# A recommender kernel on one core: each copied 256-byte row is landed as four 64-byte runs

## The chip, the cores and the metric

The kernel runs on one core of a Trainium2 chip. The metric is the device time of one execution in microseconds (us), the median of several runs. A core has five engines with a queue each: TensorE (PE), VectorE (DVE), ScalarE (ACT), GpSimd (POOL) and SyncE (SP). DMAs are issued from the queues of SP, ACT and POOL and are carried out by 16 DMA engines that all of them share.

## What is computed

```python
x = relu(dense @ Wb0 + bb0)            # dense: 2048 x 13, Wb0: 13 x 512
x = relu(x @ Wb1 + bb1)                # 512 x 256
d = relu(x @ Wb2 + bb2)                # 256 x 64
sp = emb[arange(26)[None, :], sparse_idx]      # 26 tables of 12500 rows of 64 floats
T = concatenate([sp, d[:, None, :]], axis=1)   # 27 vectors of 64 for each sample
Z = einsum('bnd,bmd->bnm', T, T)
h = concatenate([d, Z[:, li, lj]], axis=1)     # the 351 pairs below the diagonal
h = relu(h @ Wt0 + bt0)                # 415 x 512
h = relu(h @ Wt1 + bt1)                # 512 x 256
p = sigmoid(h @ Wt2 + bt2)             # 2048 outputs
```

All of it is in float32. Each sample reads 26 rows of 256 bytes from places in device memory that its indices name: 2048 x 26 = 53,248 rows.

## The kernel before

**Steps.** The batch is worked off in eight steps of 256 samples. The tile `rows` has 128 partitions; a partition holds two samples of the step (halves h = 0 and 1, 64 floats each) for each of 26 tables.

**Gathers.** Tables 0 to 24 are fetched by POOL with indirect DMAs. One takes a table and a half, 128 rows (`gather`, L376 to L380), so a step has 50 and the kernel 398 in all, issued one behind the other. `begin` holds a run of gathers until TensorE has read what it overwrites.

**Copied rows.** Table 25 (`FETCHED`) is fetched row by row with plain DMAs whose source address is read from the tile `fetch_at`: the SP queue copies the 128 rows of half 0 of a step (L335 to L341), the ACT queue those of half 1 (L758 to L764). Each copy is 256 bytes into one partition of `fetched`. A step's 128 rows on a queue are issued as four parts of 32; ahead of a part stands `keep_pace`, a wait that holds the part of number n until the gathers have come to about column 11 n (50 columns to a step), and `load_places`, a load of 32 addresses into registers (L288). `fetched` has a place of its own for each of the eight steps. DVE moves a step's 128 x 128 block into `rows` (`move_fetched`, L833 to L838) once all 256 rows have landed.

**The last step** is cut finer, so that little is left to do once the last gather lands. Half 0 of all tables comes first, with table 24 of half 1, then half 1 of tables 0 to 15 (`LAST_RUNS`). Of half 1 of tables 16 to 23 there are eight "late" tiles of 128 rows, numbered l = 0 to 7 = 2q + k, q being a quarter of the samples. Six of them are gathered by POOL (L402 to L406). The two with q = 2, `COPIED_Q`, that is l = 4 and l = 5, are copied row by row instead: l = 4 by the SP queue (L343 to L348), l = 5 by the ACT queue (L766 to L771), in four parts of 32 each and without `keep_pace`, from the time that step 6 has been transposed. They land straight in `rows`.

**TensorE** transposes what has landed (`turn` L444, `turn_last` L467, `turn_late` L479), DVE (in the last step ACT too) spreads the transposed vectors into `vecs_st` and `vecs_mv` (`spread` L844, `spread_last` L849, `spread_late` L853 and L718), TensorE forms the 27 x 27 products (L494, L510, `gram_quarter` L529), DVE transposes and packs the pairs (L871 to L886), and TensorE carries them through the top layers (L561 to L609). The PE order at the end of the last step is written out by hand: `turn_late(0)`, `turn_late(1)`, `gram_quarter(0)`, `turn_late(2)`, `turn_late(3)`, `gram_quarter(1)`, `turn_late(4)`, `turn_late(5)`, `turn_late(6)`, and so on, with filler matmuls (`stay_busy`, L539) between. `turn_late(l)` also waits for the spread of the tile two before it. DVE's order there is `spread_last(11)`, then `spread_late(1)`, (3), (5), (7); ACT has the even ones.

Of the kernel before, what the change touches and what calls it, by code (L numbers as in the profile page):

```python
# [34 lines left out]
U8 = mybir.dt.uint8  # L35

P = 128
# [3 lines left out]
DIM = 64  # L41
# [4 lines left out]
STEPS = BATCH // STEP  # L46
# [22 lines left out]
FETCHED = TABLES - 1  # L69
# [5 lines left out]


ROW_BYTES = 4 * DIM
PARTS = 4
PART = P // PARTS

# [14 lines left out]
COPIED_Q = 2  # L95
# [22 lines left out]
def build(nc, x, idx, fetch_idx, emb, wb0, bb0, wb1, bb1, wb2, bb2, wt0, wt1, bt1, wt2, bt2, out):  # L118
# [3 lines left out]
    with ExitStack() as ctx:  # L122
        def sb(name, shape, dt=F32):
            return ctx.enter_context(nc.sbuf_tensor(name, shape, dt))
# [4 lines left out]
        def sem(name):  # L129
            return ctx.enter_context(nc.semaphore(name))  # L130
# [23 lines left out]
        fetch_neg = sb("fetch_neg", [2 * PARTS, (STEPS + 1) * PART], I32)  # L154
        fetch_at = sb("fetch_at", [2 * PARTS, (STEPS + 1) * PART], I32)
        late_fetch_base = sb("late_fetch_base", [2 * PARTS, PART], I32)
        fetched = sb("fetched", [P, STEPS, 2 * DIM])

        x_t = sb("x_t", [DENSE, BATCH])
        hb0 = sb("hb0", [P, B0 // P, CHUNK])  # L160
# [37 lines left out]
        fetch_idx_loaded = sem("fetch_idx_loaded")  # L198
        fetch_done = sem("fetch_done")
        fetch_landed = [[sem(f"fetch_landed{h}_{i}") for i in range(STEPS)] for h in range(2)]  # L200
        late_fetch_landed = [sem(f"late_fetch_landed{k}") for k in range(LATE_TILES)]
        late_fetch_base_ready = sem("late_fetch_base_ready")
        fetched_moved = sem("fetched_moved")
# [70 lines left out]
        def late_rows(q, k):  # L274

            return rows[:, LATE + LATE_TILES * q + k, :]
# [16 lines left out]

        def late_landing(k, p):

            return late_rows(COPIED_Q, k)[p:p + 1, DIM:].bitcast(U8)

        def landing(i, h, p):
            return fetched[p:p + 1, i, h * DIM:(h + 1) * DIM].bitcast(U8)

        turned_tiles = [bank[0:PAIR_ROWS, 0, :] for bank in (ps_feat[1], ps_turn[0], ps_turn[1])]

# [20 lines left out]
        @block.sync  # L323
        def _(sp):
            sp.dma_start(idx_raw[:, 0:STEP_COLS], idx[:, 0:STEP_COLS]).then_inc(idx_loaded, 16)
            sp.dma_start(fetch_raw[:, :], fetch_idx).then_inc(fetch_idx_loaded, 16)
            sp.dma_start(idx_raw[:, STEP_COLS:], idx[:, STEP_COLS:]).then_inc(idx_rest_loaded, 16)
            sp.dma_start(wb0_sb[:, :], wb0).then_inc(bottom_loaded, 16)
            sp.dma_start(wb1_sb[:, :, :], wb1.rearrange("(k p) n -> p k n", p=P)).then_inc(bottom_loaded, 16)
            sp.dma_start(wb2_sb[:, :, :], wb2.rearrange("(k p) n -> p k n", p=P)).then_inc(bottom_loaded, 16)  # L330
            sp.dma_start(wt0_sb[:, :, :], wt0.rearrange("k p n -> p k n")).then_inc(top_loaded, 16)
            sp.dma_start(wt1_sb[:, :, :], wt1.rearrange("(k p) n -> p k n", p=P)).then_inc(top_loaded, 16)

            sp.wait_ge(fetch_done, 5)
            for i in range(STEPS):  # L335
                for q in range(PARTS):
                    keep_pace(sp, i * PARTS + q)
                    places = load_places(mybir.EngineType.SP, 0, q, i)
                    for j in range(PART):
                        sp.dma_start(landing(i, 0, q * PART + j), emb_bytes[bass.ds(places[j], ROW_BYTES)])\  # L340
                            .then_inc(fetch_landed[0][i], 16)  # L341

            sp.wait_ge(rows_turned, STEPS * NR)  # L343
            for jj in range(4):
                places = load_places(mybir.EngineType.SP, 0, jj, STEPS)
                for j in range(PART):
                    sp.dma_start(late_landing(0, jj * PART + j), emb_bytes[bass.ds(places[j], ROW_BYTES)])\
                        .then_inc(late_fetch_landed[0], 16)  # L348

            sp.wait_ge(probs_ready, 1)  # L350
            sp.dma_start(out.rearrange("(p n) -> p n", p=P), probs[:, :]).then_inc(out_stored, 16)
            sp.wait_ge(out_stored, 16)
# [56 lines left out]
        def _(pe):  # L409
# [60 lines left out]
            def turn_late(l):  # L470

                q, tile = LATE_RUNS[l]
                k = LAST_NR + l
                if q == COPIED_Q:
                    pe.wait_ge(late_fetch_landed[tile], 16 * P)
                else:
                    pe.wait_ge(late_landed[l], 16)
                wait_spread(k - 2)
                nc.tensor.transpose(ps_turn[k % 2][:, 0, :], late_rows(q, tile), ident[:, :]).then_inc(rows_turned, 1)  # L479
# [235 lines left out]
        def _(act):  # L715
# [42 lines left out]
            for i in range(STEPS):  # L758
                for q in range(PARTS):
                    keep_pace(act, i * PARTS + q)  # L760
                    places = load_places(mybir.EngineType.Activation, 1, q, i)
                    for j in range(PART):
                        act.dma_start(landing(i, 1, q * PART + j), emb_bytes[bass.ds(places[j], ROW_BYTES)])\
                            .then_inc(fetch_landed[1][i], 16)  # L764

            act.wait_ge(rows_turned, STEPS * NR)  # L766
            for jj in range(4):
                places = load_places(mybir.EngineType.Activation, 1, jj, STEPS)
                for j in range(PART):
                    act.dma_start(late_landing(1, jj * PART + j), emb_bytes[bass.ds(places[j], ROW_BYTES)])\  # L770
                        .then_inc(late_fetch_landed[1], 16)  # L771

            last_step()
# [7 lines left out]
        def _(dve):  # L781
# [51 lines left out]
            def move_fetched(i):  # L833

                for h in range(2):
                    dve.wait_ge(fetch_landed[h][i], 16 * P)
                dve.wait_ge(rows_turned, i * NR + NR)
                nc.vector.tensor_copy(rows[:, FETCHED, :], fetched[:, i, :]).then_inc(fetched_moved, 1)  # L838

            def spread(i, r):  # L840

# [108 lines left out]
            def last_step():  # L950
                i = STEPS - 1
                spread_last(0)
                place_d_last()
                relu_low(i - 1, 0)
                relu_high(i - 1, 0)
                spread_last(1)
                spread_last(2)
                logit(i - 1, 0)
                relu_low(i - 1, 1)
                relu_high(i - 1, 1)  # L960
                spread_last(3)
                spread_last(4)
                logit(i - 1, 1)
                copy_d_last()
                move_fetched(i)
                spread_last(5)
                spread_last(6)
                turn_gram(i, 0)
                pack(i, 0)
                spread_last(7)  # L970
                move_feat(i, 0)
                spread_last(8)
                relu_low(i, 0)
                spread_last(9)
                relu_high(i, 0)
                spread_last(10)
                logit(i, 0)
                spread_last(11)
                spread_late(1)
                spread_late(3)  # L980
                spread_late(5)
                spread_late(7)
                turn_gram_last()
                pack_last()
                move_feat_last()
                relu_high(i, 1, top_0_blocks_last(1))
                logit(i, 1)
# [112 lines left out]
```

## Time and profile before

| | us |
|---|---|
| median of 3 runs | 526.32 |
| lowest and highest | 524.11 and 526.5 |
| the profiled execution's own time | 525.22 |
| its span in the trace | 523.5 |

Busy shares of the span: POOL 72%, PE 60%, DVE 49%, ACT 1%. The 16 DMA engines move 32 GB/s in the mean. Shares are means over stages; what an edit is worth is read from the chain that ended last and from who waits for whom in the stage that it touches. The sequencers' own time (issuing DMAs, loading registers) is not counted as busy and is read by line.

### The profile page before, as it was taken

To read this page: it belongs to the slowest core of one execution; us is meant where nothing else is said; L and a number is where in the kernel's file an instruction comes from. 1 tells how busy PE (TensorE), PEld (TensorE's weight loads), DVE (VectorE), ACT (ScalarE), POOL (GpSimd) and SP (SyncE) were. 2 spreads that over 40 slices of the span, in tenths; PEclk is the share of its full clock that TensorE was granted. 3 is DMA by queue.
4 is the path that set the end of the run, shared out by engine and by line. 5 is a ranking of instruction groups with operands and counts; after the bars stand their busy time and mean duration, and the time that the engine had idled before them with its cause. 6 is when DMAs were issued, how large, how long until landed. Compare 5 with 4: busy or idle time off the path is not lost.

```text
span 523.5 us, 12507 instructions
## 1 busy us (share of the span) xinstructions
PE 315.0 (60%) x3386; PEld 230.2 (44%) x3386; DVE 254.3 (49%) x391; ACT 4.7 (1%) x11; POOL 377.6 (72%) x405
## 2 busy tenths in 40 slices
PE   3799983764372655561555834638438445497887
PEld 1233433652271535441354622626237233486765
DVE  5433866782463434822357344543446433543423
ACT  1000000000000000000000000000000000000001
POOL 5777777777777777777777777777777777777730
PEclk9978996695576765866558665676657676779589
DMA  6445324444354432454324443444323443333410
GB/s 210 33 27 30 28 30 28 30 28 28 30 29 29 27 30 28 29 28 28 28 29 28 29 27 29 27 29 29 27 28 29 27 30 29 27 27 30 31 16 3
DMA packets 20412, 16.87 MB, mean 32 GB/s; under 512 B 12163, under 2 KB 13452, under 8 KB 20345
## 3 DMA queue, kind: packets, MB, share of 16 engines
q0 software_dynamic: 12736, 13.07, 31.6%
q1 hardware_dynamic: 4634, 2.72, 4.3%
q10 hardware_dynamic: 2988, 0.54, 3.3%
q14 instruction: 42, 0.34, 0.3%
q8 instruction: 12, 0.20, 0.2%
HBM read 16.28 MB, written 0.01 MB: 31 GB/s over the span
## 4 chain that ended last, share of the span: by engine, by line
POOL 64%; issue 22%; PE 9%; DMA 2%; DVE 2%; POOLq 0%; ACT 0%; DVEq 0%; ACTq 0%
POOL rows L378 64%; PE ps_t L422 3%; DMA rows<-in_emb,idx_row 2%; PE ps_turn L430 1%; PE ps_feat L539 1%; PE ps_feat L413 1%; PE ps_gram L413 1%; DMA idx_raw<-in_idx 1%; PE ps_gram L529 1%; DVE hb L786 1%; PE ps_t L609 0%; PE ps_turn L479 0%; PE ps_t L561 0%; DVE vecs_mv L1030 0%; PE ps_feat L561 0%
## 5 line engine op out<-in xcount | busy, mean ns | idle before, releaser
L378 POOL DMA_INDIRECT rows<-in_emb,idx_row x392 | 370.1, 944 | 122.6 <-issue 119.0
L444 PE MATMUL ps_turn<-ident,rows 128*128 128x128 f32 x182 | 39.9, 358 | 140.0 <-DMA rows<-in_emb,idx_row 131.2
L844 DVE COPY vecs_st<-ps_turn 128x512 f32<-128x512 f32 (+1 forms) x49 | 47.0, 959 | 107.3 <-PE ps_turn L444 106.9
L844 DVE COPY vecs_mv<-ps_turn 64x512 f32<-64x512 f32 (+1 forms) x98 | 96.1, 981 | 0.7
L444 PEld LDWEIGHTS ps_turn<-ident,rows 128*128 128x128 f32 x182 | 25.9, 177 | 153.9 <-issue 145.6
L494 PE MATMUL ps_gram<-vecs_mv,vecs_st 128*32 128x54 f32 x1792 | 42.7, 286 | 29.3 <-DVE vecs_mv L844 15.2
L494 PEld LDWEIGHTS ps_gram<-vecs_mv,vecs_st 128*32 128x32 f32 x1792 | 39.3, 164 | 34.1 <-DVE vecs_mv L844 18.0
L609 PE MATMUL ps_t<-wt_sb,ht_t 128*128 128x256 f32 x128 | 51.3, 570 | 0.0
L609 PEld LDWEIGHTS ps_t<-wt_sb,ht_t 128*128 128x128 f32 x128 | 34.9, 286 | 15.1 <-issue 8.1
L878 DVE STREAM_TRANSPOSE gram_s<-ps_gram 128x864 f32<-128x864 f32 x15 | 16.2, 1083 | 49.5 <-PE ps_gram L494 42.2
L588 PE MATMUL ps_t<-feat_t,wt_sb 117*128 117x128 f32 x180 | 36.7, 362 | 0.2 <-DVE feat_t L890 0.2
L588 PEld LDWEIGHTS ps_t<-feat_t,wt_sb 117*128 117x128 f32 x180 | 34.6, 280 | 0.5 <-DVE feat_t L890 0.5
L422 PE MATMUL ps_t<-hb,wb_sb 128*128 128x512 f32 x64 | 32.1, 659 | 3.1 <-DVE hb L786 3.1
L588 PE MATMUL ps_feat<-feat_t,wt_sb 117*128 117x128 f32 x180 | 25.2, 276 | 0.0
L588 PEld LDWEIGHTS ps_feat<-feat_t,wt_sb 117*128 117x128 f32 x180 | 23.0, 195 | 0.0
L422 PEld LDWEIGHTS ps_t<-hb,wb_sb 128*128 128x128 f32 x64 | 13.3, 214 | 22.0 <-issue 17.3
L570 PE MATMUL ps_feat<-ident,feat 128*117 128x128 f32 x45 | 11.1, 366 | 17.6 <-DVE feat L886 17.6
L905 DVE SCALAR_TENSOR_TENSOR ht_w<-ps_t,wt_sb 128x256 f32<-128x256 f32 x16 | 6.8, 425 | 25.0 <-PE ps_t L609 25.0
L599 PE MATMUL ps_t<-bt_sb,ones 1*128 1x256 f32 x32 | 16.9, 621 | 0.0
L570 PEld LDWEIGHTS ps_feat<-ident,feat 128*117 128x117 f32 x45 | 7.7, 233 | 20.4 <-DVE feat L886 19.5
L582 PE MATMUL ps_t<-d_t,wt_sb 65*128 65x128 f32 x60 | 16.6, 372 | 0.0
L582 PEld LDWEIGHTS ps_t<-d_t,wt_sb 65*128 65x128 f32 x60 | 15.0, 292 | 1.0
(86 smaller groups left out, 238.2 us busy)
## 6 DMA issues: line engine op xcount, KB each, us to landing
fetched<-in_emb SPq DMA_DIRECT2D x1024, 0.2 KB
fetched<-in_emb ACTq DMA_DIRECT2D x1024, 0.2 KB
rows<-in_emb,idx_row POOLq DMA_INDIRECT x398, 3.7
rows<-in_emb SPq DMA_DIRECT2D x128, 0.2 KB
rows<-in_emb ACTq DMA_DIRECT2D x128, 0.2 KB
wt_sb<-in_wt SPq DMA_DIRECT2D x1, 1024.0 KB
wb_sb<-in_wb SPq DMA_DIRECT2D x1, 512.0 KB
wt_sb<-in_wt SPq DMA_DIRECT2D x1, 512.0 KB
```

The source lines that it names most:

```text
L378: nc.gpsimd.indirect_dma_start(rows[:, t, h * DIM:(h + 1) * DIM], None, emb_rows, bass.IndirectOffsetOnAxis(idx_row[:, c:c + 1], 0)).then_ ...
L413: nc.tensor.matmul(ps_b0[m], wb0_sb[:, m * P:(m + 1) * P], x_t[:, bass.ds(c * CHUNK, CHUNK)], start=True, stop=True).then_inc(b0_summed, 1)
L422: summed = nc.tensor.matmul((ps_t0, ps_t1)[m][:, :], wb1_sb[:, k, m * P:(m + 1) * P], hb0[:, k, :], start=(k == 0), stop=(k == B0 // P - 1))
L444: turned = nc.tensor.transpose(ps_turn[r % 2][:, j, :], rows[:, first + j, :], ident[:, :])
L494: summed = nc.tensor.matmul(ps_gram[32 * v:32 * v + 32, b, g * 2 * VECS:(g + 1) * 2 * VECS], vecs_st[:, c, :], vecs_mv[:, c, :, :].rearran ...
L570: turned = nc.tensor.transpose(ps_feat[u][0:PAIR_ROWS, k, :], feat[:, u, k * PAIR_ROWS:(k + 1) * PAIR_ROWS], ident[:, :])
L582: nc.tensor.matmul(top_0_blocks(u, m // 2)[:, m % 2, :], wt0_sb[0:D_ROWS, PAIR_TILES, m * P:(m + 1) * P], d_t[:, u, :], start=True, stop=F ...
L588: summed = nc.tensor.matmul(top_0_blocks(u, m // 2)[:, m % 2, :], wt0_sb[0:PAIR_ROWS, k, m * P:(m + 1) * P], feat_t[:, u, k, :], start=Fal ...
L599: nc.tensor.matmul(ps_t1[:, 0:T1], ones[0:1, :], bt1_sb[:, :], start=True, stop=False)
L609: summed = nc.tensor.matmul(ps_t1[:, 0:T1], ht0_t[:, k, :], wt1_sb[:, k, :], start=False, stop=(k == T0 // P - 1))
L844: moved = nc.vector.tensor_copy(to, source)
L878: nc.vector.transpose(gram_s[u][:, 0:VECS * SLOTS], unit_products(VECS)).then_inc(gram_turned, 1)
```

## The change

A copied row is described to the DMA as four pieces of 16 floats (64 bytes). In `fetched` a sample's row used to be one run of 64 floats; now the tile is laid out piece, half, 16 floats, so that the four pieces of one row stand 32 floats apart. `move_fetched` puts them back into order while it moves them. The late rows used to land in `rows` directly; now they land in a tile of their own, `late_copied`, in which the pieces of the two tiles alternate, and DVE moves each tile into `rows` with a copy of its own (`move_late_copied`), placed between `spread_late(3)` and `spread_late(5)`. `turn_late` of the two tiles waits for that move in place of the landing.

```diff
+PIECES = 4
+PIECE = DIM // PIECES
...
-        fetched = sb("fetched", [P, STEPS, 2 * DIM])
+        fetched = sb("fetched", [P, STEPS, PIECES, 2, PIECE])
+        late_copied = sb("late_copied", [P, PIECES, LATE_TILES, PIECE])
...
-            return late_rows(COPIED_Q, k)[p:p + 1, DIM:].bitcast(U8)
+            return late_copied[p:p + 1, :, k, :].bitcast(U8)
...
-            return fetched[p:p + 1, i, h * DIM:(h + 1) * DIM].bitcast(U8)
+            return fetched[p:p + 1, i, :, h, :].bitcast(U8)
+
+        def table_row(place):
+            return emb_bytes[bass.ds(place, ROW_BYTES)].rearrange("(o q e) -> o q e", o=1, q=PIECES)
...
-                        sp.dma_start(landing(i, 0, q * PART + j), emb_bytes[bass.ds(places[j], ROW_BYTES)])\
+                        sp.dma_start(landing(i, 0, q * PART + j), table_row(places[j]))\
                             .then_inc(fetch_landed[0][i], 16)
...
-                    sp.dma_start(late_landing(0, jj * PART + j), emb_bytes[bass.ds(places[j], ROW_BYTES)])\
+                    sp.dma_start(late_landing(0, jj * PART + j), table_row(places[j]))\
                         .then_inc(late_fetch_landed[0], 16)
...
-                    pe.wait_ge(late_fetch_landed[tile], 16 * P)
+                    pe.wait_ge(late_moved, tile + 1)
...
-                nc.vector.tensor_copy(rows[:, FETCHED, :], fetched[:, i, :]).then_inc(fetched_moved, 1)
+                nc.vector.tensor_copy(rows[:, FETCHED, :].rearrange("p (h q e) -> p q h e", h=2, q=PIECES),
+                                      fetched[:, i, :, :, :]).then_inc(fetched_moved, 1)
+
+            def move_late_copied():
+
+                for k in range(LATE_TILES):
+                    dve.wait_ge(late_fetch_landed[k], 16 * P)
+                    nc.vector.tensor_copy(late_rows(COPIED_Q, k)[:, DIM:].rearrange("p (q e) -> p q e", q=PIECES),
+                                          late_copied[:, :, k, :]).then_inc(late_moved, 1)
...
                 spread_late(1)
                 spread_late(3)
+                move_late_copied()
                 spread_late(5)
                 spread_late(7)
```

The ACT queue's two loops are changed as those of SP are.

## Rows read from the trace of the kernel before

**Rows 1.** The page's chain of work that ended last, shares of the span.
```profile
POOL 64%; issue 22%; PE 9%; DMA 2%; DVE 2%; POOLq 0%; ACT 0%; DVEq 0%; ACTq 0%
```

**Rows 2.** POOL's gathers in the costliest groups: count, busy, mean ns, idle before.
```profile
L378 POOL DMA_INDIRECT rows<-in_emb,idx_row x392 | 370.1, 944 | 122.6 <-issue 119.0
```

**Rows 3.** The same chain in order of time, near its end: start, length, what.
```profile
487.72 1.23 POOLq L122
496.74 8.17 DMA rows<-in_emb,idx_row
```

**Rows 4.** Timeline of the last step: start, length, engine, line, [idle before].
```profile
477.75 0.20 DVE L838 COPY rows<-fetched 128x128 f32<-128x128 f32 x1
...
478.92 1.47 DVE L849 COPY vecs_st<-ps_turn 64x512 f32<-64x512 f32 x2 [0.96 <-PE ps_turn L467]
...
501.73 0.95 POOL L405 DMA_INDIRECT rows<-in_emb,idx_row  x1 [0.30 <-issue]
...
501.82 0.66 PE L467 MATMUL ps_turn<-ident,rows 128*128 128x128 f32 x4 [0.21 <-DMA rows<-in_emb,idx_row]
...
502.51 1.02 DVE L849 COPY vecs_st<-ps_turn 64x512 f32<-64x512 f32 x1 [1.33 <-PE ps_turn L467]
...
504.96 0.33 PE L479 MATMUL ps_turn<-ident,rows 128*128 128x128 f32 x1 [1.14 <-DMA rows<-in_emb,idx_row]
...
508.40 0.38 DVE L853 COPY vecs_st<-ps_turn 64x128 f32<-64x128 f32 x1 [2.70 <-PE ps_turn L479]
...
509.95 0.44 PE L479 MATMUL ps_turn<-ident,rows 128*128 128x128 f32 x2
...
510.43 0.38 DVE L853 COPY vecs_st<-ps_turn 64x128 f32<-64x128 f32 x1 [1.65 <-PE ps_turn L479]
```

**Rows 5.** Gathers of L378 issued in 440 to 450 us: issue to landing.
```profile
DMA to landing us min/median/max: 3.3/3.8/4.0
```

**Rows 6.** The late gathers of L405: issue to landing.
```profile
DMA to landing us min/median/max: 6.3/8.0/8.6
```

**Rows 7.** DMA queues over the whole span: packets, MB, share of 16 engines.
```profile
q0 software_dynamic: 12736, 13.07, 31.6%
q1 hardware_dynamic: 4634, 2.72, 4.3%
q10 hardware_dynamic: 2988, 0.54, 3.3%
```

**Rows 8.** DMA queues in 452 to 456 us (q1 is SP's, q10 ACT's).
```profile
q1 hardware_dynamic: 24, 0.00, 0.5%
q10 hardware_dynamic: 22, 0.00, 0.4%
```

**Rows 9.** DMA queues in 484 to 488 us.
```profile
q10 hardware_dynamic: 19, 0.00, 5.5%
q1 hardware_dynamic: 19, 0.00, 5.3%
```

**Rows 10.** DMA queues in 504 to 512 us.
```profile
q10 hardware_dynamic: 4, 0.00, 0.0%
```

**Rows 11.** SP's and ACT's copies of the step rows: ns min/median/max, first and last start.
```profile
L340 SPq DMA_DIRECT2D fetched<-in_emb x1024: 227/228/482, 8.4 to 447.2; - x171
L763 ACTq DMA_DIRECT2D fetched<-in_emb x1024: 234/235/547, 8.6 to 447.6; - x171
```

**Rows 12.** ACT's copies in 436 to 448 us and, by L770, 449 to 462 us.
```profile
L763 ACTq DMA_DIRECT2D fetched<-in_emb x32: 234/235/468, 437.1 to 447.6; - x32
L770 ACTq DMA_DIRECT2D rows<-in_emb x32: 234/235/467, 450.2 to 461.1; - x32
```

**Rows 13.** ACT's copies of late rows in 486 to 501 us.
```profile
L770 ACTq DMA_DIRECT2D rows<-in_emb x38: 234/235/468, 485.8 to 500.3; - x38
```

**Rows 14.** SP queue, first 12 us: loads of whole tensors.
```profile
0.82 0.42 SPq L325 DMA_DIRECT2D idx_raw<-in_idx  x1
1.31 0.35 SPq L326 DMA_DIRECT2D fetch_raw<-in_fetch_idx  x1
1.71 0.35 SPq L327 DMA_DIRECT2D idx_raw<-in_idx  x1
```

**Rows 15.** Loads on ACT's queue, SP's first copied row, and the store of the output.
```profile
3.00 0.45 ACTq L750 DMA_DIRECT2D bt_sb<-in_bt  x1
3.48 0.42 ACTq L751 DMA_DIRECT2D wt_sb<-in_wt  x1
...
L340 SPq DMA_DIRECT2D fetched<-in_emb x1: 306/306/306, 8.4 to 8.4; - x1
...
521.59 0.39 SPq L351 DMA_DIRECT2D out<-probs  x1
```

**Rows 16.** DVE's move of the copied rows, all eight.
```profile
L838 DVE COPY rows<-fetched x8: 203/212/453, 85.1 to 477.8; 128x128 f32<-128x128 f32 x8
```

**Rows 17.** SP queue's waits, whole span: total, times, longest.
```profile
SPq L288 <- DMA rows<-in_emb,idx_row: 31.2, 8, 7.2
```

More of the change, by code:

```diff
@@ L200, in build @@
         fetch_landed = [[sem(f"fetch_landed{h}_{i}") for i in range(STEPS)] for h in range(2)]
+        late_moved = sem("late_moved")
         late_fetch_landed = [sem(f"late_fetch_landed{k}") for k in range(LATE_TILES)]
@@ L762, in _ @@
                     for j in range(PART):
-                        act.dma_start(landing(i, 1, q * PART + j), emb_bytes[bass.ds(places[j], ROW_BYTES)])\
+                        act.dma_start(landing(i, 1, q * PART + j), table_row(places[j]))\
                             .then_inc(fetch_landed[1][i], 16)
@@ L769, in _ @@
                 for j in range(PART):
-                    act.dma_start(late_landing(1, jj * PART + j), emb_bytes[bass.ds(places[j], ROW_BYTES)])\
+                    act.dma_start(late_landing(1, jj * PART + j), table_row(places[j]))\
                         .then_inc(late_fetch_landed[1], 16)
```

## The prediction

> **What bounds the kernel now.** First the page's chain of waits [rows 1]: 64% of the span is POOL at work and 22% "issue", the gap between two of its instructions. The groups [rows 2] give the period: 944 ns busy and 119.0 / 390 = 305 ns of gap, 1.249 us for a gather. 398 of them make 497 us, and the last starts at 501.73 [rows 4]. So up to about 502 us the time is POOL's, and it waits for no landing. A cheaper or dearer copied row can't move that stretch. What it can move is the end.
>
> The chain near its end [rows 3] goes from POOL to one gather, issued at 496.74, that lands 8.17 us later; that is `turn_late(1)`, at 504.96 [rows 4]. From there on TensorE and its helpers set the pace. Two things lie ahead of it: how late the gathers of the last step land, and whether the copied rows are there in time. Gathers need 3.8 us in the median in an undisturbed stretch [rows 5], but 8.0 at the end [rows 6]. That is the one visible cost of the present state.
>
> Why? The queues' own windows tell. In 452 to 456 us the copies make 24 + 22 packets [rows 8]. A row every 0.34 us (10.5 us for 31 rows [rows 12]) makes 12 rows a queue, so a row is two packets, data and completion. They take 0.9% of 16 x 4 us, 0.58 us, 13 ns each. In 484 to 488 us [rows 9] 38 packets take 10.8%, 6.9 us, 182 ns each, and each of the two queues is then busy 3.4 to 3.5 of the 4 us, like one lane that is nearly full. 19 rows in 4 us is 4.75 rows/us where 6 are issued: a backlog grows on that lane, and a gather, which needs all its engines, lands late because of it. The state comes and goes.
>
> **What the change does to the DMA engines.** It puts four short data pieces and four completions where one of each was. What counts is the load of the lane that is full. If four lanes do it, each gets one data packet and one completion for each row, just as the one does now. Only the size of the data packet shrinks, 256 to 64 bytes. In the quick window the mean packet, big and small, takes 13 ns [rows 8], so bytes can be worth at most a few ns of the 182: the slow window's price is for the packet, not its bytes. So I expect engine 0 as full as before and three others like it. A gather then waits for the latest of four lanes and not for one. Bounds: relief of all the delay (8.2 to 3.8 us, below) or a later landing. For the latter I take 0.5 to 1 us in `turn_late(1)`, an estimate: an eighth to a quarter of the 4.4 us by which landings are late now, since the lanes get their rows in step; up to 4.4 us if the delay doubles.
> The Trainium skill ("DMA: Bandwidth & Descriptors", "Why a DMA increments its semaphore by 16 and not by 1") says that a DMA from SP or ACT uses the lowest-numbered k engines, k being the largest number up to 16 that divides both slowest dims, each with a completion write of its own. By that, k goes from 1 to 4, engine 0 keeps a share of every row, and the copied rows' packets go from 2 to 8. The trace agrees with 2.
>
> **What it does to the queues that issue.** 1,152 copies on each of SP and ACT take 228 and 235 ns [rows 11] of a period of about 340. If a four-lane copy costs x more to issue, first the spare time eats it. ACT is the tighter one. Its rows begin at 8.6 and its late rows at 450.2 [rows 11, 12]: 441.6 us for 32 parts. A part without a wait is 13.1 us (437.1 to 450.2 [rows 12]), 32 make 419 to 421, so some 21 us are waits. SP has 31.2 us of waits [rows 17]. 21 / 1,024 rows: up to 20 ns a row the late rows still start on time. Then come 128 late rows. The last is issued at 500.3 [rows 13], four packets are left after 504 us [rows 10], so it has landed by about 505. It is needed when `spread_late(3)` ends at 508.78 [rows 4]: 3.8 us of cover. Together 21 + 3.8 = 25 us over 1,152 rows: **the cover lasts to x = 21 ns**, and beyond that every ns costs 1.15 us of the end.
>
> What is x? The trace has no four-lane copy from a warm queue. Nearest rows: the third load of SP, 128 partitions, takes 0.35 us, and the one before it with 8 partitions as much [rows 14]; against 228 ns that is at most 120 ns for 15 more lanes, 8 a lane, 24 ns for three. The store of the output, 0.39 us after a long wait [rows 15], less the 228 of a copy row and the 78 ns that the queue's first row costs above that (306 ns [rows 15]), leaves 84 ns, 17 for three lanes. ACT's one-partition load takes 0.45 us and the 128-partition one behind it 0.42 [rows 14, 15], so 0 ns. And 8 and 16 lanes cost the same [rows 14]: little hangs on the count. I take 10 ns, between the ends 0 and 40 (the jump from one lane to 8 taken whole, 120 ns, for a third of it). 10 ns x 1,024 = 10 us vanish in the waits, 1.3 us in the cover: 0 at the end.
> The Trainium skill (the same page and section, in its table of issue costs) gives 512 sequencer cycles for a copy instruction before the newest generation, with no term for the lanes; by that x would be 0. No run here shows cycles.
>
> **DVE.** `move_fetched` costs 212 ns in the median [rows 16]. Reordered in runs of 16 floats I allow 0.2 to 0.45 us. In the last step DVE ends it at 477.95 and idles until 478.92 [rows 4]: 0.96 us of cover; in the steps before, DVE is 49% busy and POOL sets the pace. The two new moves are half as large each, 2 x 0.1 to 2 x 0.3 us, after 508.78. TensorE wants them at 509.95 and DVE is next needed at 510.43 [rows 4]: 1.2 us of cover. Gone if copies land after 509.4. Removed is nothing from the end: the two late tiles were not what anybody waited for.
>
> **The sum.** POOL 0; issuing 0 (hidden up to 21 ns a row); DVE 0; later landings +0.5 to +1, taken as 0.6. Against the profiled execution, 525.22 (span 523.5 and 1.7 around it), that is 525.8; the median of the runs is 526.32, 1.1 above the profiled one, and by it the time is 526.9, rounded to 526.8.
>
> **Rivals.**
> *The issue cost breaks the cover* (slower). Place: ACT's queue, then `turn_late(4)`. It decides from x = 21 ns on: x = 30 gives +10 us (537), 40 gives +21 (548), 100 gives +90 (616). For it: 24 ns from [rows 14] is just past the point, and the margin is thin for a cost that is paid 1,152 times. Against: equal prices for 8 and 16 lanes, ACT's two equal loads. A measurable loss (over 0.5%, 2.6 us) needs x over 23. Chance 0.30.
> *The lane's load really falls* (faster). If a short piece goes through in a fraction of the time, gathers land after 3.8 us also at the end. Then `turn_last(5)`'s 6.4 us landing shrinks and DVE's wait of 0.96 goes; `turn_last(11)` gains 0.21 [rows 4]; `turn_late(1)` no longer waits for its landing but for `spread_last(11)`, which ends at 503.53, so it starts 1.43 us sooner. Sum 2.6 us: 523.7, and no more, since `gram_quarter(0)` and all behind it is TensorE's own chain. For it: 8.0 against 3.8 us. Against: 182 ns is paid by packets of any size. Chance 0.14, of which 0.08 by more than 0.5%.
> The Trainium skill's rule "Use all 16 engines" (the same page, "Rules for kernel authors") is on this rival's side; its "Specifications" speak against the change, as runs under 512 bytes are below line rate. By the trace the copies move too few bytes (31 to 32 GB/s in all) for a rate to matter.
> *Four full lanes hurt* (slower). With 48 instead of 12 packets a us, if their handling has a common limit, the copies' backlog grows on all four and late rows land after 509.4, or gathers after 10 us instead of 8: `turn_late(1)` 2 to 6 us later, 529 to 533. For it: the slow state exists at 12 packets a us. Against: in 452 to 456 the same number goes through at 13 ns. Chance 0.08 beyond 0.5%.
> *It isn't split at all*: the row is still one copy on one lane. Then only DVE's work is new: 526.3. Against: the pieces lie 128 bytes apart in the tile and can't be one run. Chance 0.05.
>
> **Chances and range.** Hidden, within 0.5%: 0.43, with the unsplit case 0.05 and the smaller reliefs 0.06: same 0.54. Faster 0.08. Slower 0.30 + 0.08 = 0.38. 0.5% is about what these runs can tell from no change. The likeliest is 526.8, its own range 525 to 529. The range runs from the full relief, 523.6, to x = 39 ns, 546, which leaves out some 0.12 above and 0.04 below.
>
> **What would show it.** Right, by [rows 7]: packets of ACT's queue 2,988 + 1,152 x 6 = 9,900 and of SP's 4,634 + 6,912 = 11,546; POOL's period 1.249 us; copies at 230 to 250 ns; SP's waits down from 31 us by about 10; late gathers still at 8 us or more; the moves under 0.3 us and ended before 509.9. Wrong by issuing: copies over 258 ns, no waits left for ACT, late rows issued past 504 us, and TensorE waiting for DVE's moves. Wrong by relief: late gathers at about 4 us and `turn_late(1)` at 502.5 or sooner. Wrong by burden: gathers of 10 us, or a long time from the last issue to the moves.

## The result, and the profile after

The changed kernel takes 994.55 us (median of 4 runs, 994.01 to 995.92), the kernel before beside it 525.83 (4 runs). The ratio is 1.893, with a 95% interval of 1.888 to 1.898. 526.8 with a range up to 546 was forecast: the forecast was wrong, in size and in which case it took for the likeliest. The rival "the issue cost breaks the cover" came true, with a price nine times the 39 ns at which my range ended.

The page of the changed kernel, its chain of work that ended last, by engine and by line (L347 is SP's copy of a step row, L354 that of a late row, L292 the load of the addresses; "SPq" is the queue of SP):

```profile
SPq 62%; issue 23%; PE 4%; another core or an unknown queue 4%; POOL 3%; DVE 2%; DMA 1%; ACT 0%; ACTq 0%; DVEq 0%
SPq L347 47%; SPq L354 8%; SPq L292 6%; POOL rows L385 3%; PE ps_gram L501 1%; DVE vecs_mv L859 1%; DMA fetched<-in_emb 1%; PE ps_t L616 1%; PE ps_feat L546 0%; PE ps_t L595 0%; PE ps_turn L474 0%; DVE vecs_st L859 0%; DMA idx_raw<-in_idx 0%; PE ps_feat L595 0%
```

POOL led the chain before [rows 1]; now it is the queue of SP, by 62%. Its copies by line, the columns as in [rows 11]:

```profile
L347 SPq DMA_DIRECT2D fetched<-in_emb x1024: 3/621/1212, 8.2 to 870.3; - x171
...
L770 ACTq DMA_DIRECT2D fetched<-in_emb x1024: 3/645/1439, 8.3 to 856.4; - x171
...
L354 SPq DMA_DIRECT2D late_copied<-in_emb x128: 576/642/711, 873.7 to 974.1; - x128
```

Before, the same instruction took 228 and 235 ns and the step rows were all issued by 448 us. Now the median is 621 and 645 ns and the last late row goes out at 974.1. POOL has turned from the bound into one that waits, as its group shows, and DVE waits 303.7 us for rows to move:

```profile
L385 POOL DMA_INDIRECT rows<-in_emb,idx_row x392 | 370.5, 945 | 425.3 <-issue 422.3
...
L845 DVE COPY rows<-fetched 128x128 f32<-128x128 f32 x8 | 1.8, 227 | 303.7 <-DMA fetched<-in_emb 303.7
```

A gather still costs 945 ns; its idle time before has gone from 122.6 [rows 2] to 425.3 us. The trace names no releaser for it ("issue"); by the kernel a step's first gathers may not overwrite `rows` until TensorE has read it, and TensorE waits 309.7 us in all for DVE's moves of table 25, about as much as the gathers have lost. So the loss isn't at the end alone. The last gather, at 501.73 before [rows 4], is now issued 303 us later:

```profile
L412 POOL DMA_INDIRECT rows<-in_emb,idx_row x6: 940/944/944, 798.6 to 804.8; - x6
```

The timeline at the end shows what is late:

```profile
966.81 0.75 PE L536 MATMUL ps_gram<-vecs_st 64*32 64x27 f32 x64
975.85 0.30 DVE L852 COPY rows<-late_copied 128x64 f32<-128x64 f32 x2 [9.40 <-DMA late_copied<-in_emb]
976.10 0.69 PE L486 MATMUL ps_turn<-ident,rows 128*128 128x128 f32 x2 [8.53 <-DVE rows L852]
```

TensorE does nothing for 8.5 us until DVE has moved the two late tiles, and DVE had waited for their last row. From there the kernel needs 16 us more.

The DMA queues of the changed kernel, over the whole span, stand beside [rows 7]:

```profile
q1 hardware_dynamic: 11546, 2.73, 1.3%
q10 hardware_dynamic: 9900, 0.56, 0.6%
```

These are exactly the packet counts forecast. The copy is split four ways, and yet the packets take less time than before: 0.6% of 16 x 992.3 us over 9,900 is about 10 ns each, where [rows 7] gives 3.3% of 16 x 523.5 us over 2,988, 93 ns. So the DMA side got better, at half the rows in a microsecond, and the six late gathers land after 2.5 us where they took 8.0 [rows 6]. The loss is in issuing.

### The profile page after: what moved, and what is told of

The parts are those of the page before. It is cut to its first block, busy times and chain, and to the rows that moved or that the text cites. A ratio compares the mean times of both kernels' runs of the same rounds, so it can differ in the third digit from the quotient of the medians.

```text
span 992.3 us, 12509 instructions
## 1 busy us (share of the span) xinstructions
PE 343.1 (35%) x3386; PEld 239.8 (24%) x3386; DVE 253.5 (26%) x393; ACT 4.7 (0%) x11; POOL 377.9 (38%) x405
## 3 DMA queue, kind: packets, MB, share of 16 engines
q1 hardware_dynamic: 11546, 2.73, 1.3%
## 4 chain that ended last, share of the span: by engine, by line
SPq 62%; issue 23%; PE 4%; another core or an unknown queue 4%; POOL 3%; DVE 2%; DMA 1%; ACT 0%; ACTq 0%; DVEq 0%
SPq L347 47%; SPq L354 8%; SPq L292 6%; POOL rows L385 3%; PE ps_gram L501 1%; DVE vecs_mv L859 1%; DMA fetched<-in_emb 1%; PE ps_t L616 1%; PE ps_feat L546 0%; PE ps_t L595 0%; PE ps_turn L474 0%; DVE vecs_st L859 0%; DMA idx_raw<-in_idx 0%; PE ps_feat L595 0%
## 5 line engine op out<-in xcount | busy, mean ns | idle before, releaser
L385 POOL DMA_INDIRECT rows<-in_emb,idx_row x392 | 370.5, 945 | 425.3 <-issue 422.3
L451 PE MATMUL ps_turn<-ident,rows 128*128 128x128 f32 x182 | 33.7, 329 | 331.2 <-DVE rows L845 309.7
L501 PE MATMUL ps_gram<-vecs_mv,vecs_st 128*32 128x54 f32 x1792 | 90.0, 293 | 141.2 <-issue 92.9
L501 PEld LDWEIGHTS ps_gram<-vecs_mv,vecs_st 128*32 128x32 f32 x1792 | 60.4, 162 | 172.2 <-issue 119.8
L845 DVE COPY rows<-fetched 128x128 f32<-128x128 f32 x8 | 1.8, 227 | 303.7 <-DMA fetched<-in_emb 303.7
L616 PE MATMUL ps_t<-wt_sb,ht_t 128*128 128x256 f32 x128 | 38.1, 438 | 19.6 <-issue 18.9
L595 PE MATMUL ps_t<-feat_t,wt_sb 117*128 117x128 f32 x180 | 33.9, 341 | 0.2 <-DVE feat_t L905 0.2
L616 PEld LDWEIGHTS ps_t<-wt_sb,ht_t 128*128 128x128 f32 x128 | 25.0, 211 | 29.7 <-issue 25.2
L595 PEld LDWEIGHTS ps_t<-feat_t,wt_sb 117*128 117x128 f32 x180 | 31.3, 256 | 0.5 <-DVE feat_t L905 0.5
L536 PE MATMUL ps_gram<-vecs_st 64*32 64x27 f32 x256 | 4.2, 222 | 64.8 <-ACT vecs_st L725 64.8
L474 PE MATMUL ps_turn<-ident,rows 128*64 128x128 f32 (+1 forms) x44 | 8.2, 329 | 40.0 <-issue 40.0
L536 PEld LDWEIGHTS ps_gram<-vecs_st 64*32 64x32 f32 x256 | 3.6, 140 | 66.7 <-issue 65.9
```

Of the source, the lines that this page charges most:

```text
L385: nc.gpsimd.indirect_dma_start(rows[:, t, h * DIM:(h + 1) * DIM], None, emb_rows, bass.IndirectOffsetOnAxis(idx_row[:, c:c + 1], 0)).then_ ...
L451: turned = nc.tensor.transpose(ps_turn[r % 2][:, j, :], rows[:, first + j, :], ident[:, :])
L501: summed = nc.tensor.matmul(ps_gram[32 * v:32 * v + 32, b, g * 2 * VECS:(g + 1) * 2 * VECS], vecs_st[:, c, :], vecs_mv[:, c, :, :].rearran ...
L595: summed = nc.tensor.matmul(top_0_blocks(u, m // 2)[:, m % 2, :], wt0_sb[0:PAIR_ROWS, k, m * P:(m + 1) * P], feat_t[:, u, k, :], start=Fal ...
L616: summed = nc.tensor.matmul(ps_t1[:, 0:T1], ht0_t[:, k, :], wt1_sb[:, k, :], start=False, stop=(k == T0 // P - 1))
```

## The experiments

Theories in the order in which they came up. A: the issue price goes by lanes or pieces. B: it is one step for whatever isn't one run. C: it is paid for several places inside one partition, and stepping over partitions is quick. D: any second piece inside a partition costs it. E: only if the dim that is split over lanes lies inside a partition.

The experiments ran on four chips. On two of them the kernel before took 525 to 526 us, on the other two 859 and 866. Times are only compared beside a kernel before on the same chip, and issue times across chips only by the median of SP's late rows (L354 or its like). On the two slow chips those go out after the last gather.

### How many pieces

```diff
-PIECES = 4
+PIECES = 2
```

> Each copied row lands as two runs of 128 bytes instead of four of 64. In the changed kernel a copy takes SP 577 ns to issue when ACT is quiet, 349 ns over the 228 of the one-run copy. Theory A, the price goes by lanes (or by pieces): 349/3 = 116 ns each, so a copy takes about 345 ns, a row about 0.44 to 0.5 us and the kernel 620 to 700 us. Theory B, one step for whatever isn't a single run, however many pieces: 577 ns again and about 990 us.

```diff
-PIECES = 4
+PIECES = 16
```

> Sixteen runs of 16 bytes. Theory A (by lanes or pieces): 228 + 15 x 116 = about 1,970 ns to issue a copy, and with 1,152 of them 2,400 to 2,600 us. Theory B (one step): about 577 ns and 990 us.

```diff
-PIECES = 4
-PIECE = DIM // PIECES
+PIECES = 17
+PIECE = 3
+KEPT = PIECES * PIECE
...
-            return emb_bytes[bass.ds(place, ROW_BYTES)].rearrange("(o q e) -> o q e", o=1, q=PIECES)
+            return emb_bytes[bass.ds(place, 4 * KEPT)].rearrange("(o q e) -> o q e", o=1, q=PIECES)
```

(The moves are cut to the 51 floats, and `rows` is cleared once for table 25.)

> Seventeen runs of 12 bytes, so that only 51 of the 64 floats of a copied row are fetched (the other 13 stay as they are; the output is not the reference's). 17 has no divisor between 2 and 16, so all pieces should go to one lane: 17 data packets and 1 completion for a row. By lanes: 228 ns to issue and about 526 us. By pieces: 228 + 16 x 116 = about 2,100 ns and over 2,400 us. Theory B (one step): 577 ns and 990 us. The packet counts tell whether it was one lane: ACT's queue 684 + 1,152 x 18 = about 21,400 packets.

Measured: 1,361.78, 1,226.96 and 1,363.80 us, one run each, beside 858.66 for the kernel before on that chip, also one run. SP's late rows in the three profiles, two, sixteen and seventeen pieces:

```profile
L354 SPq DMA_DIRECT2D late_copied<-in_emb x128: 562/562/744, 1245.4 to 1341.8; - x128
```

```profile
L354 SPq DMA_DIRECT2D late_copied<-in_emb x128: 506/538/1438, 1117.4 to 1206.7; - x128
```

```profile
L355 SPq DMA_DIRECT2D late_copied<-in_emb x128: 563/564/764, 1247.2 to 1343.3; - x128
```

562, 538 and 564 ns for 2, 16 and 17 pieces, on 2, 16 and 1 lanes. The last has all 17 on one lane, as its packets tell (ACT's queue, 1,152 x 18 + 684 = 21,420):

```profile
q10 hardware_dynamic: 21420, 0.48, 0.8%
```

Theory A falls: neither lanes nor pieces set the price. B stands so far. That sixteen pieces take 135 us less than two isn't explained by it: 24 ns on 1,152 rows are 28 us, and the rest lies in the stretched steps of this chip (below).

### Over partitions instead of inside one

```diff
-            return late_copied[p:p + 1, :, k, :].bitcast(U8)
+            return late_copied[p // 4 * 4:p // 4 * 4 + 4, p % 4, k, :].bitcast(U8)
...
-            return fetched[p:p + 1, i, :, h, :].bitcast(U8)
+            return fetched[p // 4 * 4:p // 4 * 4 + 4, i, p % 4, h, :].bitcast(U8)
...
-            return emb_bytes[bass.ds(place, ROW_BYTES)].rearrange("(o q e) -> o q e", o=1, q=PIECES)
+            return emb_bytes[bass.ds(place, ROW_BYTES)].rearrange("(q e) -> q e", q=PIECES)
```

> Four runs of 64 bytes as in the changed kernel, but into four neighbouring partitions instead of four places of one partition (the rows land in the wrong samples; the output is not the reference's). Theory C, the price is that of walking inside one partition, while stepping over partitions is quick: the loads over 8 and 128 partitions took 0.35 us, so a copy takes 230 to 350 ns and the kernel 526 to 640 us. Theories A and B: 577 ns and about 990 us, as before this edit.

Measured: 875.91 us beside 858.66 on that chip, and 255 ns for a copy:

```profile
L354 SPq DMA_DIRECT2D late_copied<-in_emb x128: 252/255/299, 804.1 to 855.9; - x128
```

The same four pieces and the same packets (11,546 and 9,900), hence the same four lanes. The source is the same 256 bytes in a row, and both traces have the landing as four elements of 64 bytes; what differs is the step from one to the next, inside a partition or over partitions. With it 322 of the 349 ns by which 577 is over 228 are gone. B falls too, C stands. It was run again on a chip where the kernel before takes 526.

> The four-partition landing again (rows land in the wrong samples; the output is not the reference's), with rounds, since the chip before took 858.66 us for the kernel before and 875.91 for this. There a copy took SP 255 ns where four places of one partition took 577. If four lanes cost 27 ns a row over 228, this is ACT's 21 us of spare waits and 3.8 us of cover against 1,152 x 27 = 31 us: 4 to 10 us slower than the kernel before on a chip where that takes 526. If four lanes bring the landings of the last gathers down to 4 us, up to 2.6 us of it come back.

Measured: 547.21 us beside 525.91, ratio 1.041 (1.035 to 1.047). ACT's late rows, in the columns of [rows 12]:

```profile
L777 ACTq DMA_DIRECT2D late_copied<-in_emb x128: 259/262/736, 473.4 to 527.6; - x128
```

They start at 473.4 instead of 450.2 and end at 527.6 instead of 500.3, so the end moved 27 us in the queue and 21 in the kernel. The expectation was 4 to 10 us, because it counted with the median, 27 ns over one lane's 235. The waits and the cover are used up by the mean. ACT's 1,152 copies take 329.2 us by the sum of their durations in the trace where those of the control below take 283.0, since a tenth of them take over 300 ns, up to 1,734 (in the control 4%). That is 46 us, 40 ns a row. Less the prediction's cover of 25 us it leaves 21 us, the loss measured. So the cover is borne out as a sum; where exactly it ends, no run shows. The gathers of the end, which landed after 5.7/7.8/8.1 us in the kernel before on this chip (control below), landed after

```profile
DMA to landing us min/median/max: 3.3/3.7/4.2
```

so the relief that the second rival spoke of can be had. It had nothing to gain here, as the copied rows came later still.

### The limits of it

```diff
-PIECES = 4
+PIECES = 16
...
-            return fetched[p:p + 1, i, :, h, :].bitcast(U8)
+            return fetched[p // 16 * 16:p // 16 * 16 + 16, i, p % 16, h, :].bitcast(U8)
```

(and `late_copied` likewise)

> Sixteen pieces of 16 bytes into sixteen neighbouring partitions (rows land in the wrong samples; the output is not the reference's). Four lanes cost SP 255 ns, 27 over one lane. If that is 9 ns a lane, sixteen cost 228 + 15 x 9 = 363 ns, which is near the 348 ns of the loads over 128 partitions, a row 457 ns, and the kernel 36 x 2.2 + 1,152 x 0.46 = 610 to 680 us. If it is one step for more than one lane, 255 ns and about 547 us.

Measured: 659.42 us (one run) beside 525.44.

```profile
L354 SPq DMA_DIRECT2D late_copied<-in_emb x128: 315/369/1461, 559.1 to 627.0; - x128
```

369 ns: over partitions a lane costs 141 / 15 = 9.4 ns, as 27 / 3 = 9 for four. Set against the 538 ns of sixteen pieces inside one partition, the step costs 169 ns here and 322 with four pieces, so it isn't one fixed sum.

```diff
-            return fetched[p:p + 1, i, :, h, :].bitcast(U8)
+            return fetched[p // 2 * 2:p // 2 * 2 + 2, i, p % 2::2, h, :].bitcast(U8)
```

(and `late_copied` likewise)

> Four pieces of 64 bytes again, two in each of two neighbouring partitions (rows land in the wrong samples; the output is not the reference's). Theory D, any walk over several pieces inside a partition costs the 320 ns that lie between 577 and 255: a copy takes SP about 560 to 580 ns and the kernel 950 to 1,000 us. Theory E, the price falls only when the dim that the lanes are split over lies inside a partition: here it is the two partitions, a copy takes 237 to 260 ns, 1,152 x 9 to 1,152 x 30 ns stand against 25 us of cover, and the kernel takes 524 to 550 us.

Measured: 1,372.78 us beside 866.19, ratio 1.587 (1.581 to 1.594).

```profile
L354 SPq DMA_DIRECT2D late_copied<-in_emb x128: 612/612/811, 1252.5 to 1352.6; - x128
```

612 ns, the dearest form of all: E falls, D stands. It isn't what the lanes are split over, it is a second piece in a partition at all. Why this form is 35 ns dearer than four pieces in one partition, no run tells. Do the gaps matter?

```diff
-        fetched = sb("fetched", [P, STEPS, PIECES, 2, PIECE])
+        fetched = sb("fetched", [P, STEPS, 2, PIECES, PIECE])
...
-            return fetched[p:p + 1, i, :, h, :].bitcast(U8)
+            return fetched[p:p + 1, i, h, :, :].bitcast(U8)
```

(and `late_copied` likewise)

> The copy is described as four pieces as in the change, but they lie side by side, so that a row is one run of 256 bytes in the tile. If the pieces are then merged: one lane, 2 packets a row (2,988 on ACT's queue), 228 ns to issue, the time of the kernel before. If they are not merged: 4 lanes, 9,900 packets, 577 ns, 990 us; then it isn't the gaps that cost but any walk over more than one piece inside a partition.

Measured: 525.03 us beside 525.44, ratio 0.999 (0.997 to 1.001). 228 ns a copy and, on ACT's and SP's queues, the packets of [rows 7]: pieces that touch become one run again (in the trace, one element of 256 bytes).

```profile
L354 SPq DMA_DIRECT2D late_copied<-in_emb x128: 227/228/323, 449.3 to 497.9; - x128
```

### VectorE's part, one queue alone, and a control

```diff
-        fetched = sb("fetched", [P, STEPS, PIECES, 2, PIECE])
-        late_copied = sb("late_copied", [P, PIECES, LATE_TILES, PIECE])
+        fetched = sb("fetched", [P, STEPS, 2 * DIM])
+        late_copied = sb("late_copied", [P, LATE_TILES, DIM])
```

(with copies and moves to match, as one run each)

> Copies as one run of 256 bytes as before, but the late rows land in a tile of their own and VectorE moves them: VectorE's part of the change alone (without the reordering). Both theories of the issue cost have it equal to the kernel before within 0.3%: the two moves take 0.1 to 0.3 us and are over before TensorE wants the tiles. If the moves or the wait were part of the loss, it is slower by over 1 us.

Measured: 525.64 us beside 525.91, ratio 1.001 (0.998 to 1.003). VectorE's late moves and the new wait cost nothing that can be measured. This run leaves out the reordering; in the changed kernel a reordered move takes 227 ns where 212 [rows 16] stood before.

```diff
-                        act.dma_start(landing(i, 1, q * PART + j), table_row(places[j]))\
+                        act.dma_start(landing(i, 1, q * PART + j), emb_bytes[bass.ds(places[j], ROW_BYTES)])\
```

(ACT's late rows likewise, and tiles of their own for ACT's rows)

> SP's copies in four pieces, ACT's in one run as before. In the changed kernel SP's copy took 577 ns when ACT was quiet and about 650 with ACT issuing too. If each queue pays for itself, SP stays at 577 ns, ACT at 235, and SP's 36 parts (2.1 us of load and 32 rows of 0.67 us each) set the end: 36 x 23.6 = 850 us and about 20 behind it, 870. If the two queues share what is slow, ACT's copies rise above 235 and SP's stay above 600: 900 or more. If the sum of both counts, about 760.

Measured: 896.07 us beside 525.91, ratio 1.703 (1.696 to 1.711). SP's late rows, and ACT's step rows:

```profile
L360 SPq DMA_DIRECT2D late_copied<-in_emb x128: 576/577/622, 782.3 to 875.8; - x128
```

```profile
L776 ACTq DMA_DIRECT2D fetched<-in_emb x1024: 234/288/782, 8.6 to 617.3; - x171
```

SP stays at 577 ns, ACT's plain copies rise from 235 to 288 in the median. So each queue pays for itself, and they also hinder each other. No theory of the expectation fits whole: SP's 577 ns are the first's, ACT's dearer copies the second's, and the time lies by the second's "900 or more" rather than by the first's 870.

> The kernel before, unchanged, for its own profile beside the others. In the look before this one it took 858.66 us on the chip used, against 526 elsewhere. If that chip holds up the two issuing queues (in the four kernels profiled on it single register moves, 29 ns normally, last about 700 ns while gathers are being issued), the same stretched moves stand in this profile and the time is near 860. On a chip that does not, no move is longer than 100 ns and the time is about 526.

The control: 526.33 us beside 525.91, ratio 1.001 (0.998 to 1.004). On this chip none of SP's moves of the kernel before is longer than 29 ns:

```profile
L340 SPq MOVE fetched<-in_emb x1024: 29/29/29, 8.4 to 446.1; - x171
```

so the question put there went unanswered for the kernel before on a slow chip, which wasn't profiled. For the changed kernel and two pieces it was asked again:

> Two runs of 128 bytes, run again on a chip whose issuing queues aren't held up (on the first one its copies took 562 ns in the quick cases, but 1,362 us in all). If the price is one step whatever the number of pieces: 560 ns, SP and ACT together about 0.72 us a row, and 960 to 1,000 us in all. If the long moves of that chip are a matter of this kernel, it is at 1,360 us again.

> The changed kernel unchanged, beside the other two: 990 to 1,000 us if the first chip was a usual one. Its profile had 84 register moves of over 300 ns, 49 us in all; if those belong to the kernel they are there again, if to the chip they are not and the time is up to 49 us less.

Both ran on a slow chip again: 1,364.71 and 1,372.55 us beside 866.19, ratios 1.577 (1.570 to 1.584) and 1.586 (1.580 to 1.592). Two pieces are as dear as four. A register move and the late copies of the changed kernel there, the move from the stretch of 120 to 124 us:

```profile
L347 SPq MOVE fetched<-in_emb x1: 1395/1395/1395, 121.6 to 121.6; - x1
```

```profile
L354 SPq DMA_DIRECT2D late_copied<-in_emb x128: 576/577/695, 1255.1 to 1352.3; - x128
```

With the gathers over, a copy takes 577 ns there as elsewhere; before that, single steps of 29 ns take about 700 or 1,400. SP and ACT have 336 moves of over 300 ns in this trace, the last of them 14 us after the last gather was issued. The changed kernel on the first chip has 84 such moves as well, up to 899 ns, so they aren't the slow chips' alone.

### What do the packets cost, and can the relief be had?

```diff
+SHORT = 16
...
-            return fetched[p:p + 1, i, h * DIM:(h + 1) * DIM].bitcast(U8)
+            return fetched[p:p + 1, i, h * DIM:h * DIM + SHORT].bitcast(U8)
...
-                        sp.dma_start(landing(i, 0, q * PART + j), emb_bytes[bass.ds(places[j], ROW_BYTES)])\
+                        sp.dma_start(landing(i, 0, q * PART + j), emb_bytes[bass.ds(places[j], 4 * SHORT)])\
```

(on the kernel before; the late rows likewise)

> The kernel before, but of each copied row only 64 of the 256 bytes are fetched, in one run on one lane (the other 48 floats are left out; the output is not the reference's). In the four-partition run the last gathers landed after 3.7 us in the median where the unchanged kernel beside it had 7.8, and the copies' packets took 9 ns where the unchanged kernel's took up to 180. If it was the short packet that cured this, it is cured here too: last gathers at about 3.7 us, the copies' packets near 10 ns, and the time 1 to 3 us under the kernel before. If it was the four lanes, the gathers stay at about 8 us and the time is the same. My prediction held that bytes don't matter.

Measured: 523.34 us beside 525.44, ratio 0.997 (0.995 to 0.999). The copies' queues in 484 to 488 us, as in [rows 9]:

```profile
q1 hardware_dynamic: 22, 0.00, 0.3%
q10 hardware_dynamic: 22, 0.00, 0.3%
```

44 packets take 0.6% of 64 us, 9 ns each, on one lane, where the 38 of [rows 9] took 182 each. Its late gathers land after

```profile
DMA to landing us min/median/max: 5.6/6.2/6.7
```

The short packet cures the slow packets without any further lane. It doesn't do the same for the gathers, which were expected at 3.7 us: on this very chip, the run with the pieces together, whose copies are those of the kernel before, has

```profile
DMA to landing us min/median/max: 5.1/7.4/7.8
```

so 1.2 us are won, against 4.1 (7.8 to 3.7) with four lanes on the other chip. Slow packets are a part of the gathers' delay; whether the lanes are the rest is not shown. The gain in time is 2 us or 0.3%, and the short rows carry less data too.

The same relief was sought without short packets, by getting the copies out of the way sooner:

```diff
-PACE = 11
+PACE = 9
...
-            sp.wait_ge(rows_turned, STEPS * NR)
```

(ACT likewise; copies and moves as in the run with VectorE's part alone)

> One-run copies as before; the late rows land in a tile of their own, so that they need not wait until step 6 has been read, and the pace is set looser (9 columns a part for 11), so that both queues run through. ACT's last copy then starts at about 8.5 + 36 x 13.2 = 483 us instead of 500, and the last gathers (issued 495 to 502) meet quiet lanes. If the late landing is the copies' doing and worth what the prediction put on it, they land after 3.7 us, the start of the last tiles gains 1.4 to 1.6 us, and the time is 0.2 to 0.4% under the kernel before. If something else holds them up, the landings stay at 8 us and the time is the same.

Measured: 537.13 us beside 525.44, ratio 1.024 (1.021 to 1.026), a miss with the wrong sign. The chain in order of time tells where:

```profile
419.24 19.72 DMA rows<-in_emb,idx_row
439.27 20.45 DMA rows<-in_emb,idx_row
```

Single gathers take 20 us to land, though the median of those between 380 and 445 us is 3.6, near the 3.8 of [rows 5]. The copies were all issued by 479 us, and still their packets go on in 484 to 488:

```profile
q10 hardware_dynamic: 19, 0.00, 5.9%
q1 hardware_dynamic: 19, 0.00, 4.1%
```

So the copies have a backlog. Counted from the trace, rows issued less rows moved, it grows to 109 rows at 400 us and is gone by 500; in the kernel before, at steps of 20 us, it is never over 20. The last steps run late, though POOL issues its last gather at 502.58. The pace isn't idle time to be won: it lets the copies drain. (Pace and wait were taken out together, so their shares aren't known.) No version here that computes the reference beats the kernel before.

## Why the prediction was wrong

**"What is x?" is the step that failed.** It took 10 ns between 0 and 40, from loads of whole tensors with one piece in each of 8 or 128 partitions, and the runs showed 349. The change lands four pieces inside one partition. For pieces over partitions the rows read well: the prediction's 8 ns a lane and 24 for three against 9.4 and 27 measured. For pieces inside a partition none of the rows that I set beside it was of the kind. The price is 577 - 228 = 349 ns with ACT quiet: 27 also over partitions, and 322 for stepping inside one. The bound should have been wider, and the trace of the kernel before had a hint: SP's loads that are described as two or four pieces in each of 128 partitions (the pieces touch in the tile and lie apart in device memory).

```profile
2.54 0.38 SPq L329 DMA_DIRECT2D wb_sb<-in_wb  x1
2.97 0.51 SPq L330 DMA_DIRECT2D wb_sb<-in_wb  x1
3.52 0.52 SPq L331 DMA_DIRECT2D wt_sb<-in_wt  x1
4.08 0.51 SPq L332 DMA_DIRECT2D wt_sb<-in_wt  x1
```

Three of the four take 0.51 to 0.52 us where [rows 14] has 0.35; the first, also of four pieces, takes 0.38, so the hint is a weak one. Taken as a bound they give x = 0.29 us, and with 1.15 us for a ns beyond 21 a time over 830. A rival with that end would have had its place.

**"A cheaper or dearer copied row can't move that stretch"** failed with it. It is true inside the cover. Past it the rows of each step are late, and TensorE, then POOL, wait for them in every step: the last gather went from 501.73 to 804.81. "ACT is the tighter one" held for the kernel before; in the changed one SP ends last (974.1 against 962.2).

**The cover** (21 ns a row on average, then 1.15 us for a ns) held as a rule: a mean of 40 ns a row took the kernel to 547. With x = 349 it gives 1,152 x 0.349 - 25 = 377 us, 904 in all, near the 896 of the run in which SP alone has four pieces. So the price of one queue explains four fifths of the loss. The other 90 us come from both queues having it, which the prediction had no term for.

Counted on SP's queue: its last row moved from 498.4 to 974.1, by 476 us. With SP alone in four pieces it goes out at 875.8: (875.8 - 8.5) / 36 is 24.1 us a part against 12.7 (32 rows of 0.33 and a load of 2.1 us), so 36 x 11.4 = 410 us are its own copies. The other queue's four pieces add 974.1 - 875.8 = 98. 31 us of waits [rows 17] are gone. 410 + 98 - 31 = 477. Little of the 98 is in the copies themselves: SP's 1,024 step copies and their register moves take 635 us by the sum of their durations against 622 in the run with SP alone, 43 of the 635 in moves of over 300 ns that the other run doesn't have. Most of the 98 is time between SP's instructions for which the trace names nothing. What holds them up is open.

**"Bytes can be worth at most a few ns of the 182"** was wrong, though nothing hung on it in the end. In the window of [rows 9] rows of 64 bytes take 9 ns a packet. I had read from the quick window that size doesn't matter and carried it to the slow one. Nor are the 182 ns a lane's work on a packet: the two queues' packets add up to 6.9 us in a window of 4, more than one lane has, so they hold waiting. And "where 6 are issued" isn't so in that window: the kernel before issues 19 rows in it, as many as its 38 packets carry. So the four lanes aren't "as full as before": they are nearly empty, also with four times the packets.

**The rivals.** "The issue cost breaks the cover" was right in mechanism, at 0.30, with a price too small and a place too narrow (both queues, SP's last; then every step's move, and `turn_late(4)` only in the last). "The lane's load really falls" was right that short packets go through in a fraction of the time. Gathers after 3.8 us came with four lanes alone, and that its 2.6 us lie near the 2 measured with short rows is in part luck, since there the gathers still took 6.2. "Four full lanes hurt" and "it isn't split at all" were wrong. VectorE at nothing was right: 0.998 to 1.003 by its own run, without the reordering.

**On the Trainium skill.** Its rule on the lowest-numbered k engines ("DMA: Bandwidth & Descriptors", "Why a DMA increments its semaphore by 16 and not by 1") gives all packet counts seen, 17 pieces with one completion included; which engines they were, the counts don't show. Its table of issue costs has one figure for a copy instruction, 512 cycles, by which x would be 0. The traces have no cycles, but one figure doesn't fit what was measured: 228, 255, 369 and 577 ns on one queue, by the form of the landing.

## What to carry to other kernels

A price for a DMA's issue must come from a DMA of the same form: how many partitions it touches, and whether it has more than one run in a partition. Where a queue issues a thousand small copies, work out first how many ns each it can bear (spare waits over the count), for beyond that every ns is paid in full, and set the mean issue time against it, not the median. More lanes for a transfer are worth nothing if the queue that issues it becomes the bound; and a wait that paces a queue may be what keeps the transfers of another short.

## What the runs showed of the hardware

- Issue time of a copy on SP, median of the late rows (ACT quiet for the four-run form, 642 ns with ACT issuing such copies too): one run 228 ns; four partitions 255; sixteen 369; two, four, sixteen and seventeen runs inside one partition 562, 577, 538 and 564; two partitions with two runs each 612. Runs that touch count as one: 228.
- The packets of 256-byte rows on one lane can take 182 ns each, waiting included, where those of 64-byte rows at about the same rate take 9. Why, no run here tells.
- Two of four chips run the kernel before in 859 to 866 us instead of 526. In profiles of other kernels there, the register moves and copies of SP and ACT stretch to about 700 ns or a multiple in the part of the run that has gathers, and not after. The change costs 1.59 times there and 1.89 elsewhere. That the stretching is what makes the kernel before slow there is not shown, as it wasn't profiled there.
